# Key fills ahead of the weighing, copies from VectorE to ScalarE, and the gelu rows one place later

## The reference

```
x = x + L0_xattn(norm(x), ctx)   # norm(x) @ W1.T + mean over ctx @ W2.T + b
x = x + L0_attn(norm(x))         # 16 heads over the 64 rows, with a distance bias
x = x + L0_ffn(norm(x))          # shared silu ffn, and 8 experts, 2 of them a row
x = x + L1_xattn(norm(x), ctx)   # 16 heads, 64 queries against 1601 keys and values
x = x + L1_attn(norm(x))         # conv, gated recurrence, silu ffn, rms norms
x = x + L1_ffn(norm(x))          # weights of three values, rows of 8 bits, gelu between
```

## Time and profile before

| | |
|---|---|
| median of 3 runs | 2299.13 us (2295.34 to 2302.2) |
| the profiled execution | 2304.58 us, its span 2302.8 us |
| busy: PE, PEld | 2017.2 us (88%), 1609.4 us (70%) |
| busy: DVE, ACT, POOL | 1365.5 us (59%), 1071.7 us (47%), 559.8 us (24%) |
| mean granted TensorE clock | 0.954 of full speed |

### The profile page before, as it was taken

One profiled execution on the slowest core, in us unless ns is written; L12 is line 12 of the kernel. 1 busy time (PEld: TensorE's weight loads), 2 busy tenths in 40 slices (PEclk: granted clock), 3 DMA queues, 4 the chain that ended last, 5 costly groups with the idle time before them and its releaser, 6 DMA issues.

```text
span 2302.8 us, 73024 instructions
## 1 busy us (share of the span) xinstructions
PE 2017.2 (88%) x31670; PEld 1609.4 (70%) x31686; DVE 1365.5 (59%) x2593; ACT 1071.7 (47%) x2206; POOL 559.8 (24%) x964
## 2 busy tenths in 40 slices
PE   2698999999999988999899988999999988899964
PEld 2576777777877777777777777777777766777743
DVE  2456665656656566666656676575656566555633
ACT  2354445445454544546454544454544444444431
POOL 0222322222323121323222122231222222122210
PEclk8799999899999999999899999999999999999986
DMA  6242423242423333333232423243332302222121
GB/s 205 91 177 94 138 93 117 104 137 94 146 80 107 113 123 117 121 117 118 85 133 84 163 70 119 96 141 100 113 130 83 117 24 77 81 88 67 55 75 46
DMA packets 99116, 243.94 MB, mean 106 GB/s; under 512 B 13168, under 2 KB 19440, under 8 KB 98800
## 3 DMA queue, kind: packets, MB, share of 16 engines
q1 hardware_dynamic: 98800, 239.26, 30.7%
HBM read 235.94 MB, written 3.15 MB: 104 GB/s over the span
## 4 chain that ended last, share of the span: by engine, by line
PE 65%; DVE 18%; ACT 10%; issue 5%; SPq 1%; DMA 1%; POOL 0%; DVEq 0%; POOLq 0%; ACTq 0%
PE M L726 10%; PE SC L905 9%; PE O L951 8%; PE M L733 8%; ACT probT L1125 7%; PE SC L928 6%; PE X L755 4%; DVE mx L1429 4%; PE M L755 3%; PE SC L921 2%; PE X L1011 2%; DVE oT L1444 2%; PE M L796 2%; PE X L982 1%; PE M L760 1%
## 5 line engine op out<-in xcount | busy, mean ns | idle before, releaser
L1429 DVE TENSOR_REDUCE mx<-SC 128x4 f32<-128x1600 f32 (+1 forms) x256 | 466.5, 1822 | 193.6 <-PE SC L905 190.5
L1125 ACT ACTIVATE probT<-SC 128x512 f32<-128x512 f32 (+1 forms) x1024 | 444.9, 522 | 196.8 <-PE SC L928 193.6
L1070 ACT ACTIVATE kT<-M,bk 128x400 f32<-128x400 f32 (+1 forms) x256 | 152.9, 597 | 636.3 <-PE M L726 635.9
L594 POOL TENSOR_TENSOR rowsT<-raw,rowsT 128x384 fp32r<-128x384 f32 (+1 forms) x256 | 285.7, 1136 | 432.1 <-ACT rowsT L1175 430.9
L726 PE MATMUL M<-rowsT,wks 128*128 128x400 f32 (+1 forms) x1536 | 357.8, 369 | 10.7 <-PE O L951 9.7
L733 PE MATMUL M<-wvs,rowsT 128*128 128x256 f32 x2496 | 360.8, 293 | 1.0 <-DVE SA L1273 1.0
L733 PEld LDWEIGHTS M<-wvs,rowsT 128*128 128x128 f32 x2496 | 315.7, 192 | 25.3 <-issue 2.2
L951 PEld LDWEIGHTS O<-probT,V 128*17 128x17 f32 x13312 | 202.0, 101 | 153.5 <-issue 140.9
L905 PE MATMUL SC<-kT,bdq 32*128 32x400 f32 (+1 forms) x2048 | 257.7, 572 | 58.4 <-ACT probT L1125 43.5
L726 PEld LDWEIGHTS M<-rowsT,wks 128*128 128x128 f32 x1536 | 272.2, 192 | 40.7 <-issue 18.3
L1249 DVE TENSOR_TENSOR V<-M,bv 128x256 f32<-128x256 f32 (+1 forms) x448 | 159.6, 397 | 213.7 <-PE M L733 209.5
(11 more groups left out here) (250 smaller groups left out, 2400.5 us busy)
## 6 DMA issues: line engine op xcount, KB each, us to landing
ring<-in_ws_dram SPq DMA_DIRECT2D x428, 256.0 KB, 4.5
raw<-in_ctx_dram SPq DMA_DIRECT2D x32, 1601.0 KB, 7.2
summed<-in_ctx_dram SPq DMA_DIRECT2D x60, 800.5 KB, 4.6
ring<-rounded_scratch SPq DMA_DIRECT2D x64, 256.0 KB, 6.0
out_dram<-x SPq DMA_DIRECT2D x16, 128.0 KB, 1.7
x<-in_x_dram SPq DMA_DIRECT2D x1, 1792.0 KB, 10.7
kT<-in_ctx_dram SPq DMA_DIRECT2D x2, 800.5 KB, 8.9
rounded_scratch<-wround SPq DMA_DIRECT2D x8, 128.0 KB, 2.1
```

Source lines behind the costliest of these rows:

```text
L594: pool.tensor_tensor(rowsT[1][:, c, at], raw[:, c, at], rowsT[0][:, c, at], ALU.subtract).then_inc(low_ready, 1)
L1070: act.activation(keys(n, c)[:, k0:k0 + kn], bank[:, 0:kn], ACT.Identity, bias=bk[:, c:c + 1]).then_inc(m_used[f % 2], 1)
L1125: act.activation(probT[step % 2][0:w, j, 0:len(ts), :].rearrange("p t q -> p (t q)"), SC[0:w, j, 0:len(ts) * P], ACT.Exp)\
L1429: dve.tensor_reduce(mx[c][:, :, n], SC[:, :, 0:KCH[n][1]], AX.X, ALU.max).then_inc(max_used, 1)
```

## The change

TensorE and all drains get a new place, "middle", between `maxima` and `weigh`, with the fills of the list SECOND (key fills, and value 2 in cycle 4). The layers' fills stay in "second", behind the weighing and place C. The numbering of fills stays the same. ScalarE drains the key before it does the context sums, and place C's X fill between them.

The high part of the first piece of a batch goes from the end of cycle 7 to behind the exps of cycle 0, and the low part of it on GpSimd behind that cycle's layer work. ScalarE copies the turned maxima ahead of its exps, and the sums; VectorE takes the reciprocal from SBUF. VectorE drains ff1 behind the reduction of the maxima. hq goes from (17, "B") to (17, "D"), down from (17, "D") to (18, "B").

```diff
-        (15, "B"): "up0", (17, "B"): "hq", (17, "D"): "down"}
+        (15, "B"): "up0", (17, "D"): "hq", (18, "B"): "down"}
...
-    for what in (FIRST, SECOND)[half == "second"][k]:
+    for what in {"first": FIRST[k], "middle": SECOND[k]}.get(half, ()):
...
+def splits(b, k, places):
+
+    for piece, at in enumerate(places):
+        if k == at and 0 <= b + 1 < B:
+            yield b + 1, piece
+
+
+HIGH_AT, LOW_AT = (0, 0, 1, 3), (0, 1, 2, 4)
...
                     maxima(b, k)
+                    for what in pieces(b, k, "middle"):
+                        fill(what)
                     if k:
                         weigh(b, k - 1)
...
+                    if kind in ("max0", "max1"):
+                        act.activation(mT[n % 2][int(kind[-1])][:, :], X.bitcast(BF16)[:, 0:P], ACT.Copy).then_inc(x_used, 1)
+                    elif kind == "sums":
+
+                        if n >= 2:
+                            x_is_used(act, "out", n - 1 - n % 2)
+                        act.activation(oT[:, :, n % 2 * S:(n % 2 + 1) * S], Xg, ACT.Copy).then_inc(x_used, 1)
...
                 for b, k in SLOTS:
+                    for what in x_fills(b, k, "A"):
+                        drain_x(what)
                     if 0 <= b < B:
                         exps(b, k)
+                    for n, piece in splits(b, k, HIGH_AT):
+                        if piece == 0:
+                            high_part(n, piece)
...
                     load_table(b, k, ACT.Exp)
+                    for what in pieces(b, k, "middle"):
+                        drain(what)
+                    for what in x_fills(b, k, "C"):
+                        drain_x(what)
                     for j, c in sums(b, k):
                         context_sum(j, c)
...
-                        dve.reciprocal(oTb, Xg).then_inc(x_used, 1)
-                        x_is_used(dve, kind, n)
+                        go(dve.reciprocal(oTb, oTb))
...
                     for what in x_fills(b, k, "B"):
-                        drain_x(what)
+                        if what[0] not in ("ff1",):
+                            drain_x(what)
                     maxima(b, k)
...
+                    for what in x_fills(b, k, "B"):
+
+                        if what[0] in ("ff1",):
+                            drain_x(what)
```

More of the change, by code:

```diff
@@ L250, in count_all @@
             count(what, NUMBER, what[1], cycle)
-        for place in "BC":
-            for what in x_fills(b, k, place):
-                count(what, XNUMBER, what[0], cycle)
+        for what in x_fills(b, k, "B"):
+            count(what, XNUMBER, what[0], cycle)
+        for what in pieces(b, k, "middle"):
+            count(what, NUMBER, what[1], cycle)
+        for what in x_fills(b, k, "C"):
+            count(what, XNUMBER, what[0], cycle)
         for what in pieces(b, k, "second"):
@@ L687, in _ @@
                         split_max(b + 1, 0)
-                    for n, piece in splits(b, k, 1):
-                        low_part(n, piece)
+                    for n, piece in splits(b, k, LOW_AT):
+                        if piece:
+                            low_part(n, piece)
                     t, at = query_place(b)
@@ L1129, in drain_x @@
                     kind, n = what
-                    if kind not in ("query_in", "query", "conv_in", "gru_in", "ff_in", "hg0", "hg1", "ff0", "ff1", "ff2", "xq", "up0", "hq"):
+                    if kind not in ("max0", "max1", "sums", "query_in", "query", "conv_in", "gru_in", "ff_in", "hg0", "hg1", "ff0", "ff1", "ff2", "xq", "up0", "hq"):
                         return
                     x_is_filled(act, *what)
-                    if kind == "query_in":
+                    if kind in ("max0", "max1"):
[4 more added lines that the diff above has]
+                        act.activation(oT[:, :, n % 2 * S:(n % 2 + 1) * S], Xg, ACT.Copy).then_inc(x_used, 1)
+                    elif kind == "query_in":
                         act.activation(nqT[:, :, :], Xc, ACT.Copy).then_inc(x_used, 1)
@@ L1220, in _ @@
                         drain_x(what)
-                    for n, piece in splits(b, k, 0):
-                        high_part(n, piece)
+                    for n, piece in splits(b, k, HIGH_AT):
+                        if piece:
+                            high_part(n, piece)
             @block.vector
@@ L1437, in drain_x @@
                     kind, n = what
[L1438 to L1442, removed]
+                    if kind == "sums":
+                        x_is_used(dve, kind, n)
                         oTb = oT[:, :, n % 2 * S:(n % 2 + 1) * S]
-                        dve.reciprocal(oTb, Xg).then_inc(x_used, 1)
-                        x_is_used(dve, kind, n)
+                        go(dve.reciprocal(oTb, oTb))
                         dve.tensor_tensor(oTb, osb[:, :, :], oTb, ALU.mult).then_inc(oT_ready, 1)
@@ L1636, in _ @@
                             route(n, step)
-                    for what in x_fills(b, k, "A"):
-                        drain_x(what)
                     for what in pieces(b, k, "first"):
```

1 line of the change is left out of this document (added).

## The result

The changed kernel takes 2326.3 us (median of 4 runs, 2319.4 to 2333.9), the kernel before 2300.7 beside it: a ratio of 1.0115, 95% interval 1.0077 to 1.0154. It is slower by some 26 us; the forecast was 25 us faster, and 2326 lies above the range of 2240 to 2304.

The account below looks back on a forecast made before the run. A plain cycle's first half was taken as bound by the exps, its second by TensorE. The terms summed to -25 us: 2279.6 for the profiled 2304.6 us execution, 2274 against the median, say 2275; range 2240 to 2304.

Parts of the forecast that it names:

- the first: Key fills ahead of the weighing: order free on TensorE, first layer's scores no longer wait for the key's drain; -8.5 us.
- First high part, -9: Copy moved from cycle 7's end behind cycle 0's exps: about 31 cycles at 0.3 us; bounds 0 and -16.
- hq and down, -16: Gelu rows one place on: -11 us for TensorE's wait for quantised rows, -5 for down matmuls filling cycle 2's exps wait.
- Copies on ScalarE, -2: Maxima and sums copies: 27 us of TensorE waits gone against 25 new, from later exps and ff_in rows; bounds -27, +17.
- ff1's drain, +6: Drain behind the maxima's reduction: X given back later, ff2's fill waits 0.4 us on average in 15 cycles.
- Context sums, +14: ScalarE's sums behind the key's drain: next scores wait in cycles 2 and 0; 14 us, bounds 0 and +40.
- Clock, -10: Scored stretch: removing long TensorE waits takes away a fifth of the low clock; -10 us, bounds 0 to -25.
- Tail, +0.5: Tail of the kernel: the last sums get one copy more; +0.5 us.
- The slower case: ScalarE's queue holds a cycle through late exps, behind copies and context sums; 2312 us, chance 0.17.
- the wash: Removed waits are taken over by the next ones and the clock stays; 2297 us, chance 0.16.
- TensorE's busy time should fall by some 10 us: Sign expected in the profile after the change: TensorE's busy time down some 10 us, clock at 0.975 or above.

Follow-up runs that it names:

- without the middle: Changed kernel with SECOND's fills of key and value behind the weighing again and context sums ahead of the key's drain on ScalarE; 2281.6 us, ratio 0.9918.
- the fastest version: Changed kernel with weighing last in the cycle, context sums right behind the exps, and VectorE's ff1 drain ahead of the maxima's reduction; 2262.3 us, ratio 0.9813.
- the run without the ff1 edit: Kernel without the middle, with VectorE's drain of ff1 put back ahead of the maxima's reduction; 2283.5 us, ratio 0.9908.

## Why the prediction was wrong

**The step that failed** is the first: "TensorE's second half keeps its length, so the move itself costs nothing: the 2.45 us are the same in either order". The gain it was to bring, -8.5, came: the key's drain is gone from the waits. But the order isn't free. With the context sums' 14 taken off, the middle costs 45 - 14 = 31 us, good to some 10, so the term stood at -8.5 and measured some +31. That is 40 of the 51 us between forecast and result (2326 against 2275). Of the other 11, 10 are the clock, which I had as a term of its own and which the measured terms hold already; the misses of the smaller terms (hq and down +8, copies -6, ff1 -4) nearly cancel, in part by luck.

What stood in its place: before, a cycle went maxima, weighing (pieces of the array), key fill, layers' fills (full width), next scores (pieces). The change makes it maxima, key fill, weighing, layers' fills, scores: one more change from pieces to full width and back, in each cycle that has something behind the weighing. I counted them in the traces, as neighbouring groups of weight loads. From pieces to full width it is 538 times before, 709 after, 538 without the middle, 535 with the weighing last, and as often back; from one full-width group to another it is 546, 375, 546 and 548 times. At full clock the first load of a group starts 2 to 4 ns (median) ahead of its matmul where the kind changes, in either direction, and 108 to 118 ns ahead between two groups of full width. Two prices come out of the starts of the matmuls (medians at full clock, without idle time). From the key fill's last matmul to the next group it is 275 ns where that is the weighing and 183 where it is of full width: 0.09 us. And a full-width group takes longer from its first to its last matmul behind the weighing than behind another of its width: 320 ns for 215 (the sums' two matmuls), 883 for 778 (the eight matmuls of L1007), 165 for 108 (two transposes): 0.06 to 0.1 us. Leaving the weighing itself costs the same, 149 to 152 ns, whether full width or the scores come next. So what is lost is the place where two full-width groups were neighbours: 171 times 0.15 to 0.2 us, 26 to 34 us.

The single cycles say the same. I took the time from the maxima to the next scores in cycles in which both kernels were at full clock and did not wait. In the 26 with nothing behind key fill and weighing it is what it was (median 0 ns); in the 75 with key fill, weighing and a full-width group it is 184 ns longer (median). With the weighing last it is 1 ns longer in 73 such cycles. The order's effect is shown: in the five kernels with the weighing between groups of full width TensorE is busy 2041 to 2045 us over the whole, in the nine without it 1991 to 2027; of four executions at a mean clock of 0.958, the two with it 2041.1 and 2041.2, the two without 2013.3 and 2017.1. That the exposed load is the mechanism is read from rows and fits in size, and no run changed the load alone: whether the load waits, or the array has to finish one kind before it takes the other, these rows don't separate.

The Trainium skill ("TensorE: Matmul & The Clock Gate", Part 3, The mechanism) states that the engine pulls a weight load ahead of running matmuls when it goes to row groups that don't conflict with theirs, or to the background buffer. By that rule a full-width load behind piece matmuls needn't wait if the background buffer is free; the rows here show it waiting (262.47 and 262.48). The same section of the Trainium skill also has it that loads overlap running matmuls only when the row group differs. The weighing and the fills both use all 128 rows, so that agrees with the wait, but not with the loads between two full-width groups, which start 108 to 118 ns ahead of their matmuls. For this kernel the measurement decides.

**The other terms.**
- *First high part, -9*: measured -9.7. Right. The exps of cycle 0 start at once, and the copy behind them:

```profile
994.62 2.06 ACT L1135 ACTIVATE probT<-SC 128x512 f32<-128x512 f32 x4 [0.32 <-PE SC L936]
996.55 1.08 ACT L1192 ACTIVATE rowsT<-raw 128x1024 fp32r<-128x1024 f32 x1
996.99 0.31 PEld L913 LDWEIGHTS SC<-kT,bdq 32*128 32x128 f32 x8
997.00 0.95 PE L913 MATMUL SC<-kT,bdq 32*128 32x400 f32 x8
```

The exps start 1.36 us behind the scores (993.26), not 1.86 as in the earlier trace rows, and the maxima's 0.29 us of wait is gone.
- *hq and down, -16*: measured -8.5 (good to 7), mis-sized. The cycle that loses hq is 18.0 us shorter, the one that gets down 8.0 longer: I had down as filler of a wait (-5) and it is mostly more work in a cycle that was full.
- *Copies on ScalarE, -2*: measured -8, within the bounds, but not its size. The mechanism is there in full; in cycle 3 of batch 15, set beside the earlier trace rows:

```profile
1152.66 0.38 ACT L1149 ACTIVATE oT<-X 128x256 f32<-128x256 f32 x1 [1.05 <-PE X L986]
1152.94 1.53 ACT L1202 ACTIVATE summed<-summed 128x1601 f32<-128x1601 f32 x1
1153.08 1.75 DVE L1468 RECIPROCAL oT<-oT 128x256 f32<-128x256 f32 x1 [0.35 <-ACT oT L1149]
...
1154.46 0.27 ACT L1144 ACTIVATE mT<-X 128x128 bf16<-128x128 bf16 x1
...
1155.70 0.41 PE L969 MATMUL X<-ident,rb 128*128 128x128 f32 x2 [1.51 <-DVE rb L1519]
```

The reciprocal holds nobody's bank any more, but it starts at 1153.08, 3.40 us behind the end of the maxima (1149.68; I had reckoned with 3.65, and 1.9 before), and the rows for ff_in are late by 1.51 us. Here the context sum stands ahead of the maxima's copy too, a coupling that I had priced for the exps alone. The copy itself takes 274 ns in the mean of 64:

```profile
L1144 ACT ACTIVATE mT<-X 128x128 bf16<-128x128 bf16 x64 | 17.6, 274 | 54.9 <-PE X L980 54.5
```

My 0.3 was right. The estimate from the Trainium skill ("ScalarE: Activation LUTs", What ACT_TABLE_LOAD costs) was 293 ns, 7% above it.
- *ff1's drain, +6*: between +2 and +16 by the two runs; by the trace's own cycle 10 to 14, so it was too small, for I took half of a wait of 0.8 us in 15 cycles.
- *Context sums, +14*: measured +13.6 (good to 10) and +13 (good to 7). Right, as far as they tell.
- *Clock, -10*: the direction was right. The mean granted clock of the changed kernel's runs is 0.957, that of all 65 runs of the kernel before 0.952. By the slope of the last section this is 6 us: the means are 2326.5 and 2303.7, 23 us apart, and taken to one clock they would be 29 apart. In the two traces the low clock takes 111 us of the scored cycles before and 87 after, which is the fifth that I had forecast; but the long waits aren't shown to be the reason, as the clock of one kernel's runs scatters by more (0.943 to 0.961 before).
- *Tail, +0.5*: the tail is 0.2 us longer.

**The rivals.** The slower case was given 0.17 and the right side of the error, but for another reason: "ScalarE's queue becomes what holds a cycle". The exps' wait grew by 10 us, far from the 70 that it would have needed. So that the kernel became slower is no hit of this rival. (In the wash, 25 - 10 - 12 leaves 3, not 2.) No rival said that TensorE's own matmuls would take longer. Of the signs that the prediction named, one fell at once: "TensorE's busy time should fall by some 10 us". It rose by 28. The measured terms without the middle, -9.7, -8.5, -8 and +2, make -24, and the kernel without it stands at -19, so the parts add up to within 5 us.

## What to carry to other kernels

When matmuls on pieces of the array and matmuls on all of it share a queue, the order has a price of its own: count how often the kind changes in a cycle before and after, and keep the full-width groups next to each other. Read it in the weight loads: a load that starts with its matmul is exposed, one that starts 0.1 to 0.2 us ahead is hidden. And when a change moves blocks on the bounding engine, compare its busy time first: if that has grown for the same matmuls, no wait will explain the loss.

## What the runs showed of the hardware

*Neighbouring full-width groups are cheap.* TensorE took 0.09 us more for going from full width to pieces, 0.06 to 0.1 us more inside the full-width group that came behind the weighing, than with two full-width groups in a row (medians of the traces before, after and with the weighing last).

*The scatter of one kernel's runs goes with its clock.* Five runs of the fastest version took 2250.5, 2253.2, 2262.3, 2262.9 and 2267.1 us at mean granted clocks of 0.967, 0.964, 0.959, 0.960 and 0.955. Over the 12 experiments and 65 runs of the kernel before, a run with a clock 0.001 higher is 1.17 us shorter than others of the same kernel (from 0.8 to 1.6 in the single kernels, but for one of four runs in a narrow range), and with that taken out the scatter of the kernel before falls from 4.6 to 2.3 us. This is why a trace's cycles can be 10 us shorter and the time the same: taken to one clock, the run without the ff1 edit is 5 us faster than its partner, not 2 slower.

*Lower clock and waits don't go in step.* In the scored cycles the kernel before and the changed one are both idle for 179 us, with 111 and 87 us at the low clock; with the weighing last it is 172 us and 84 us, and in the fastest version 155 and 43. Each is one execution. I had tied the clock to the long waits of the earlier trace rows; the runs show neither a rule nor a price for that beyond the slope above.
